# Routing of tokens to experts done sequence by sequence inside self attention, into a fixed region per expert

## The reference

```
x = x + cross_attention(layernorm(x), ctx, 8 heads of 64)
x = x + self_attention(layernorm(x), 8 heads of 128, 2 latent kv groups of rank 32)
xt = layernorm(x)                              # 1024 tokens x 512
probs = softmax(xt @ Wg)                       # 8 experts
topv, topi = top_k(probs, 2); topv /= sum(topv)
moe    = sum over the two chosen experts of topv * (gelu(xt @ Wu[e]) @ Wd[e])   # F = 1024
shared = gelu(xt @ W1) @ W2
x = x + shared + moe
```

## Time and profile before

| what | us |
|---|---|
| median of three runs | 1587.81 |
| profiled execution, own time | 1589.36 |
| profiled execution, span | 1587.5 |
| PE busy | 1516.4 (96%) |
| POOL busy | 720.5 (45%) |
| ACT busy | 686.3 (43%) |
| DVE busy | 625.6 (39%) |

### The profile page before, as it was taken

How to read it: one execution, slowest core, us unless ns; L and a number is a source line. 1 busy time by engine, 2 the same in 40 slices (tenths; PEclk the granted TensorE clock), 3 DMA queues, 4 the chain that set the end, 5 groups by cost and what they waited for, 6 DMA issues and landing times. The chain is left out here.

```text
span 1587.5 us, 25168 instructions
## 1 busy us (share of the span) xinstructions
PE 1516.4 (96%) x10038; PEld 1221.4 (77%) x10039; DVE 625.6 (39%) x953; ACT 686.3 (43%) x1121; POOL 720.5 (45%) x563
## 2 busy tenths in 40 slices
PE   7999999999999999999999999888699979999997
PEld 5678888888888888888888888745367768877876
DVE  4134434533534533632732731732654522222222
ACT  3244544544543544544543643504254424444621
POOL 3113822931941841851751651537200175688651
PEclk9999999999999999999999999999899989999999
DMA  6111021021021021021111111052000475467511
GB/s 212 60 54 59 2 87 44 18 87 34 28 87 34 28 87 34 28 75 39 35 60 54 34 41 54 1 194 92 15 1 1 153 226 146 140 190 195 146 35 35
DMA packets 56164, 116.90 MB, mean 74 GB/s; under 512 B 11072, under 2 KB 15232, under 8 KB 56064
## 3 DMA queue, kind: packets, MB, share of 16 engines
q1 hardware_dynamic: 46480, 98.17, 18.6%
q0 software_dynamic: 4816, 8.41, 2.8%
q10 hardware_dynamic: 4768, 8.91, 2.0%
HBM read 94.19 MB, written 22.33 MB: 73 GB/s over the span
## 5 line engine op out<-in xcount | busy, mean ns | idle before, releaser
L282 POOL TENSOR_TENSOR ctx_l<-stage,ctx_h 128x1024 fp32r<-128x1024 f32 x62 | 147.0, 2393 | 482.3 <-ACT ctx_h L630 482.3
L344 PE MATMUL ps_p<-wv,ctx_h 128*128 128x512 f32 x1024 | 323.7, 397 | 10.4 <-DVE ctx_l L700 9.4
L344 PE MATMUL ps_p<-ctx_h,wk 128*128 128x512 f32 x1024 | 331.0, 394 | 0.0
L738 DVE TENSOR_TENSOR s_top<-ps_s,s_top 128x512 f32<-128x512 f32 x192 | 121.2, 684 | 338.8 <-ACT s L599 338.8
L344 PEld LDWEIGHTS ps_p<-wv,ctx_h 128*128 128x128 f32 x1024 | 188.0, 189 | 53.7 <-issue 10.0
L344 PEld LDWEIGHTS ps_p<-ctx_h,wk 128*128 128x128 f32 x1024 | 192.2, 188 | 42.6 <-issue 1.2
L344 PE MATMUL ps_p<-wv,ctx_l 128*128 128x512 f32 x512 | 200.4, 391 | 0.0
L344 PE MATMUL ps_p<-ctx_l,wk 128*128 128x512 f32 x512 | 199.5, 390 | 0.0
L581 ACT ACTIVATE vt<-ps_p 128x512 f32<-128x512 f32 x128 | 76.4, 598 | 274.9 <-PE ps_p L344 213.7
L599 ACT ACTIVATE s<-ps_s 128x512 f32<-128x512 f32 x256 | 133.0, 602 | 61.1 <-PE ps_s L397 36.7
L575 ACT ACTIVATE kT<-ps_p 128x512 f32<-128x512 f32 x128 | 76.5, 598 | 176.7 <-PE ps_p L344 176.6
(11 more groups left out here) (255 smaller groups left out, 2253.9 us busy)
## 6 DMA issues: line engine op xcount, KB each, us to landing
stage<-in_ctx_dram SPq DMA_DIRECT2D x64, 512.0 KB, 4.0
raw_u<-in_up_dram SPq DMA_DIRECT2D x32, 512.0 KB, 4.2
stage<-in_down_dram SPq DMA_DIRECT2D x16, 512.0 KB, 4.1
raw_e<-in_down_dram SPq DMA_DIRECT2D x16, 512.0 KB, 4.1
rows_scratch<-wxo SPq DMA_DIRECT2D x25, 256.0 KB, 2.6
wxo<-rows_scratch ACTq DMA_DIRECT2D x23, 256.0 KB, 3.3
s<-in_x_dram SPq DMA_DIRECT2D x2, 1024.0 KB, 11.5
q_scratch<-s SPq DMA_DIRECT2D x2, 1024.0 KB, 4.6
```

The lines of the kernel that those rows point to most:

```text
L282: nc.gpsimd.tensor_tensor(lo, raw, hi, ALU.subtract).then_inc(done, 1)
L344: mm = nc.tensor.matmul(out, w(c), m(c), start=(c + k == 0), stop=(c == DC - 1 and k == 2))
L738: ins = nc.vector.tensor_tensor(top[:, p, e], bank, top[:, p, e], ALU.max)
```

## The change

- `EARLY` is 6, with a lag of its own: in step s the first half of shared tile `s - 1` and the second half of tile `s - 2` run, so tiles begin in step 1 where they began in step 3. `keys(1)` and `latents(1)` move to step 0. More raw buffers for the shared weights (parts of `wq`) keep the gelu's buffer free.
- A class `Routing` does the routing of sequence s - 1 in step s; the last sequence's is done in `experts`. The running counts are summed on POOL (`heap`).
- Each expert has a region of eight blocks of 128 rows in `rows_dram`, so a slot is `128 * 8 * expert + rank`. Two indirect DMAs per sequence send rows of 517 numbers: the 512 channels, the token, two weights, two experts. The 16 DMAs of tags and their table are gone. A table `where_i` maps tile number to block; ACT reads it for each load, DVE copies the tags out of the loaded rows (`take_tags`) and picks the weight (`choose_weight`).
- Cross attention fills all 66 blocks (517 wide, token number 1024), ten at the end of each b, from a buffer `blank`.
- The softmax's multiplication by the inverse sum moves from DVE (two instructions per sequence) to ACT (eight).
- The identity and the two masks for the ranks are set in self attention, not at the start of `experts`.

```diff
-ROWS = MAX_TILES + 2
+REGION = B * T // P
+ROWS = E * REGION + 2
-EARLY = 4
+EARLY = 6
+LAG = 1
@@ cross attention, SP
-                for n in range(B * T // P + (b - 1) * ZB, min(B * T // P + b * ZB, ROWS)):
-                    sp.dma_start(rows_dram[n], wxo[:, 0, :]).then_inc(zeroed, 16)
+                for n in range((b - 1) * ZB, min(b * ZB, ROWS)):
+                    sp.dma_start(rows_dram[n], blank[:, :]).then_inc(zeroed, 16)
@@ self attention, POOL, step s
                 if s < 2:
                     split(CH - 2 + s)
+                if s:
+                    routing.count(pool, s - 1)
+                    routing.scatter(pool, s - 1)
@@ self attention, PE
+            def rank(s):
+                await_empty(pe, f"rk{s}")
+                if s == 0:
+                    pe.wait_ge(on_set, 8)
+                pe.wait_ge(routing.both_done, s + 1)
+                pe.wait_ge(routing.heap_done, s + 1)
+                nc.tensor.matmul(bank(f"rk{s}")[:, 0:E], before, routing.both[:, s, :], start=True, stop=False)
+                fill(nc.tensor.matmul(bank(f"rk{s}")[:, 0:E], ones, routing.heap[:, s, :], start=False, stop=True),
+                     f"rk{s}")
@@ PE, step s
-                late, soon = s - EARLY, s - EARLY + 1
+                late, soon = s - LAG - 1, s - LAG
                 turn_probs(s)
                 if s + 1 < B:
                     scores(s + 1)
-                if late >= 0:
+                if 0 <= late < EARLY:
                     turn_gelu(late)
...
                 mix(s)
-                if late >= 0:
+                if s:
+                    rank(s - 1)
+                if 0 <= late < EARLY:
                     down_high(late)
                 if 0 <= soon < EARLY:
                     turn_norm(f"rowT{soon}", soon, B + soon + 1)
+                if s == 0:
+                    keys(1)
                 self_out(s)
-                if s == 1:
-                    keys(1)
-                if s == 2:
+                if s == 0:
                     latents(1)
@@ ACT, step s
                 take(f"pT{s}0", pT[:, 0])
+                if s:
+                    routing.exps(act, s - 1)
...
                 if s + 1 < B:
                     exps(s + 1)
...
+                if s + 1 < B:
+                    normalise(s + 1)
                 take(f"x3T{s}", x3T[:, s % 2])
@@ DVE, step s
                 if s + 1 < B:
                     maxes(s + 1)
+                if s:
+                    routing.choose(dve, s - 1)
                 take(f"u{s}", uT[:, :, :])
...
+                if s + 1 < B:
+                    invert(s + 1)
                 add(f"wo{s}", s)
...
                 norm(s, B + s)
-                if s + 1 < B:
-                    normalise(s + 1)
+                if s:
+                    await_filled(dve, f"rk{s - 1}")
+                    copy(nc.vector.tensor_tensor(routing.place[:, :], bank(f"rk{s - 1}")[:, 0:E], routing.base[:, :], ALU.add),
+                         f"rk{s - 1}")
+                    await_copied(dve, f"rk{s - 1}")
+                    routing.place_rows(dve, s - 1)
...
+                routing.largest(dve, s)
@@ class Routing: choose = max, max_index, copy of the two indices, compare,
@@ compare and add (both_done), then sum, reciprocal and multiply of the weights;
@@ place_rows = two picks, a reduce, a cast (slots_done)
+    def scatter(self, pool, s):
+        pool.wait_ge(self.tags_done, s + 1)
+        pool.wait_ge(self.slots_done, s + 1)
+        for k in range(2):
+            pool.indirect_dma_start(
+                out=self.rows_dram.rearrange("n p d -> (n p) d"),
+                out_offset=bass.IndirectOffsetOnAxis(ap=self.slot_i[:, k, s:s + 1], axis=0),
+                in_=self.xn3[:, s, :], in_offset=None).then_inc(self.added, 16)
@@ experts, SP
             load_raw(1)
-            sp.wait_ge(tags_set, 1)
-            sp.dma_start(meta_dram.rearrange("(p r) w -> p r w", p=P), pad[:, :, :]).then_inc(padded, 16)
-            for t in range(NT - 2):
-                store_out(t)
-            load_raw(2)
-            for t in range(NT - 2, NT):
+            for t in range(EARLY):
                 store_out(t)
             sp.wait_ge(added, 16 * 2 * NT)
-            sp.dma_start(tag[:, 0:MAX_TILES, :], meta_dram.rearrange("(r p) w -> p r w", p=P)).then_inc(tags_in, 16)
+            sp.dma_start(row[:, :], rows_dram[0]).then_inc(row_in, 16)
+            load_raw(2)
+            for t in range(EARLY, NT):
+                store_out(t)
@@ experts, POOL (the 32 indirect DMAs of rows and tags before are gone)
+            routing.scatter(pool, NT - 1)
@@ experts, PE: rank_last stands between the high and the low part of the up layer of tile 6
-            pe.wait_ge(consts, 9)
             turn(EARLY, xn3[:, EARLY, :])
-            tile(EARLY, 0, 0, rank_hits)
+            tile(EARLY, 0, 0, rank_last)
@@ experts, ACT
             def load_row(n):
-                act.dma_start(row[:, :], rows_dram[bass.ds(n, 1)].rearrange("o p d -> (o p) d")).then_inc(row_in, 16)
+                place = act.value_load(where_i[0:1, bass.ds(n, 1)], min_val=0, max_val=ROWS - 1)
+                act.wait_ge(tag_taken, n)
+                act.dma_start(row[:, :], rows_dram[bass.ds(place, 1)].rearrange("o p d -> (o p) d")).then_inc(row_in, 16)
@@ experts, DVE, tile 7 and routed tiles
+            weights_rest(range(DC))
+            hidden_rest(NT - 1)
+            row_rest(NT)
+            weights_rest(range(DC, CH))
+            dve.wait_ge(row_in, 16 * NT + 16)
+            take_tags(NT)
+            add_shared(NT - 1)
...
                 with dve.Fori(*bounds(dve, e)) as t:
+                    dve.wait_ge(row_in, t * 16 + 32)
+                    take_tags(t + 1)
                     hidden_rest(t)
                     row_rest(t + 1)
+                    choose_weight(t, e)
```

More of the change, by code:

```diff
@@ L1371, in exps, with normalise @@
                     copy(ins, f"sc{s}{g}")
+            def normalise(s):
+                par = s % 2
+                for g in range(SKV):
+                    act.wait_ge(inv_done, s * SKV + (g + 1))
+                    for r in range(REP):
+                        ins = nc.scalar.activation(sm[:, par, g, r, :], sm[:, par, g, r, :], ACT.Copy,
+                                                   scale=inv[:, par, g, r:r + 1])
+                    ins.then_inc(p_done, 1)
             for n in range(2):
@@ L1532, in experts @@
+def experts(nc, room, stage, on, up_ap, down_ap, out_ap, rows_dram, x2, xn3, logits, hu0, hd0, lu0, ld0,
+            rowT_h, rowT_l, gT_h, gT_l, raw_in, hi_done, lo_done, routing, added):
     with ExitStack() as ctx:
@@ L1573, in experts @@
         first_i = sb("first_i", [P, E + 1], U32)
-        slot = sb("slot", [P, 2, NT])
-        slot_i = sb("slot_i", [P, 2, NT], U32)
+        SEEN = MAX_TILES + 2
+        gap = sb("gap", [P, E - 1])
+        number = sb("number", [P, SEEN])
+        where = sb("where", [P, SEEN])
+        where_i = sb("where_i", [P, SEEN], U32)
+        passed = room[:, 0, 0:SEEN * (E - 1)].rearrange("p (t e) -> p t e", e=E - 1)
+        iota = routing.iota
         up_ps = ctx.enter_context(nc.psum_tensor("up_ps", [P, NH, 512], F32))
@@ L1829, in round_weights, with tile @@
                         .then_inc(hi_done, 1)
-            def tile(t, before_load=None):
+            def tile(t):
                 for n in range(NH):
@@ L1847, in _ @@
             act.sem_inc(row_in, 16 * NT)
-            act.wait_ge(route, 2)
-            nc.scalar.activation(probs[:, :, :], probs[:, :, :], ACT.Exp).then_inc(e_done, 1)
+            routing.exps(act, NT - 1)
             round_row(EARLY)
@@ L1852, in _ @@
             round_weights(1, None)
[L1853 removed]
+            for t in range(EARLY + 1, NT):
+                if t + 1 == NT:
+                    act.wait_ge(where_done, 1)
                 tile(t)
[L1856 to L1857 removed]
             act.wait_ge(firsts_done, 1)
@@ L1930, in _ @@
-            link(nc.vector.memset(first[:, 0:1], float(NT)))
-            hidden_rest(EARLY)
-            row_rest(EARLY + 1)
-            dve.wait_ge(counted, 1)
-            for t in range(NT):
-                link(nc.vector.tensor_tensor(earlier[:, t + 1, :], total_ps[:, t * E:(t + 1) * E], earlier[:, t, :],
-                                             ALU.add))
-            link(nc.vector.tensor_tensor(full[:, :, :], earlier[:, NT, :].unsqueeze(2).broadcast_to([P, E, NT - 1]),
+            dve.wait_ge(counted, 1)
```

376 lines of the change are left out of this document (210 added, 166 removed).

## The result

The changed kernel takes 1593.91 us, the median of 6 runs (1592.77 to 1595.16), against 1587.8 us of the kernel before beside it: a ratio of 1.0039, 95% interval 1.0026 to 1.0052. It is slower by more than the 0.2% that can be told. I had forecast 1576.3 us and a range up to 1587: both are wrong, and so is the side. On another chip the same two kernels gave 1594.66 and 1588.36 us, 1.0042 (1.0029 to 1.0055), so the loss is not that of one chip. The profiled execution took 1593.26 us with a span of 1591.4, where I had worked out 1577.9 and 1576.0.

A forecast was written before the change was run, and what follows sets the result against it. TensorE, busy 96% of the span, was taken as the bound, with a wait for tile 8's rows. The turn behind tile 8 was put at 1305.3, not 1316.86: 1587.81 - 11.5 = 1576.3 us; forecast 1571 to 1579, wider range 1563 to 1587.

The forecast's parts named there:

- Cross attention: Writing 66 blocks instead of 25 was to cost 0, with 7 us for each of six sequences as upper bound.
- Step 0: First step of self attention, with keys(1), latents(1) and ACT's eight multiplications: 18.0 us, from 15.5.
- The wait at the rank: Steps 2 to 6: TensorE stands 1.45 us for DVE's choose ahead of the rank matmuls; 20.4 us per step, from 18.70.
- Tile 8's rows in time: In experts, the rows of tile 8 land likeliest 22.5 us after the block's start, against 23.6 needed: no wait.
- rival B: Tile 8's rows come late in experts, with a wait of up to 6.5 us: 1579 to 1585 us; chance 0.15.
- Rival C: The new stop ahead of down_high drops the clock, 3 us lost each time; 1597 us with seven falls; chance 0.09.
- Step 1: Second step of self attention, with tile 0's up layer in and choose on the path: 18.8 us, from 16.2.
- Step 7 and the block's end: From step 7's start to the first turn of experts 15.6 us, TensorE starting at once after POOL's last scatter.
- Behind tile 8: In experts, expert 2's late weight chunks delay tile 8's gelu by 1.9 us; next turn 14.3 us later.
- The rest: Per routed tile, ACT's register read and DVE's tags and weight choice: 0, bounded by 0.3 us for each of 21 tiles.
- The mechanism of the gain: In experts, the 9.0 us wait for tile 8's rows goes, and 2.4 us of slow restart with it.
- rival A: The rank wait is filled or the early steps' clock lifted, up to 8.7 us back: 1565 to 1570 us; chance 0.20.

The follow-up runs named there:

- Experiment 1: Changed kernel, with DVE copying tile 8's tags ahead of the low parts of weight chunks 4 to 7: 1594.38 us.
- experiment 2: Changed kernel, with the weight choice's two scalar_tensor_tensor written as tensor_scalar; run twice, on two chips: second run 1592.35 us, 1.0018 to the kernel before.
- experiment 3: Changed kernel, with sequence 6's scatter issued at the start of experts, not at the end of self attention; run twice: second run 1592.18 us, 1.0017 to the kernel before.
- experiment 5: Changed kernel, with ACT normalising sequence 1 ahead of the copy of the values' second half in step 0: 1593.79 us, 1.0039 to the kernel before.
- experiment 6: Changed kernel, with the choice of experts behind the reciprocals on DVE and the rank matmuls behind the output matmuls: 1584.05 us, 0.998 to the kernel before.
- experiment 7: Changed kernel with all five edits (those of experiments 1, 2, 3, 5 and 6), run on two chips: 1577.08 us (0.993) and 1577.50 us (0.9927).
- the control: The changed kernel itself, unedited, timed again beside experiments 5 to 7 on another chip: 1594.66 us, 1.0042 to the kernel before.
- experiment 4: Changed kernel, with the two rank matmuls moved on TensorE from ahead of down_high to behind the row turn: 1593.74 us.

## Why the prediction was wrong

**Right.** Cross attention costs nothing. Step 0 (17.85 for 18.0; ACT's eight multiplications took 2.43 us for the 2.7 counted). The wait at the rank: 1.30 us for the 1.45 worked out, steps of 20.51 for 20.4. Tile 8's rows in time, rival B being wrong. Rival C, a fall of the clock in every step, is wrong too: the five waits of 1.30 us brought none (1.00 in the window of step 2; all of experiments 1 to 3 and 5 show one case), though it had the right side and was off by only 3 us in the time.

**Wrong, in four terms, all of them too small.**

*Step 1, 18.8.* "Followed operation by operation this gives 18.8 us": the text names no stretch of it at the lower clock. Its rank wait was 2.48 us, not 1.45, for there is no `down_high` and no tile before it. Windows show the clock at 0.50 from 1130 to 1136, behind the two waits of step 0, and again near 1140 to 1142 (0.53 from 1140 to 1143). In the kernel of experiment 6 with waits of 1.03, 1.24, 1.10 and 1.09 us and no second fall, the step took 19.71 us. With nearly the same waits ahead of a fall, in experiment 7, it took 22.01. One kernel shows it by itself: that of experiment 2 took 21.82 us in step 1 in its first trace and 24.42 in its second, where the second fall lasted longer and the clock fell a third time (0.61 from 1148 to 1152, 1.00 in the first trace). The first traces of experiments 1 and 3, whose edits don't touch step 1, have 24.40 and 24.42. So falls of the clock move step 1 by 2.3 to 2.6 us, with nothing changed in the work. The second fall of the changed kernel was a short one: TensorE is busy for 16.90 us of the step, 15.24 in experiment 6. So about 1.7 of the 3.3 us are the clock and 1.0 the longer rank wait; the rest is not taken apart.

*Step 7 and the block's end, 15.6.* "TensorE then starts at once": I let the block end with POOL's last instruction, 1.2 us behind the others. It ended 3.0 us behind POOL's last indirect DMA, and the experts started at the lower clock all the same. Experiment 3 took away 3.4 of the 3.9 us.

*Behind tile 8, 1.9 charged.* I followed the chunks, and not what stands ahead of the rounding in ACT's queue: a row load with a new wait, for a copy of DVE that stands behind 4.6 us of low parts. The tags are part of the change; my text had them under "the rest", at no charge. Experiment 1 puts 1.7 us on them, and leaves the other 1.9 to the chunk transfers that I had named and made too short.

*"The rest. ... I charge 0."* I had reasoned by room: DVE waits 4 us for each tile. It had the room, but an operation with two SBUF inputs, which the forecast had made one of "three small operations", stood for up to 5.15 us beside POOL's subtractions, past the end of the down layer. Experiment 2 gives back 2.5 of the 3.6 us.

The mechanism of the gain was right: the wait for tile 8's rows goes, and the turn of these rows comes 12.46 us behind the one before it, for 21.42. What made the side wrong is the sum: 14.4 us in these four terms, none of them the rank's wait of steps 2 to 6, which I had counted. Those five steps were also the largest cost of all, and the wait in them wasn't necessary. I took DVE's fixed order as a bound ("its order is fixed, with maxes first") and so gave rival A, a filled wait, as something that might happen by itself; it needed an edit, which gave 10.6 us in all, 5.1 of them in steps 2 to 6. That the kernel with all five edits comes out at 1577 us, near the forecast, is no support for the forecast: it lacks the rank waits that the forecast had in it.

What stays open: why the kernel before took 10 us more on one chip and whether the change loses there, and what decides whether the clock falls behind a wait of 1.1 us in step 1. With two to three us hanging on such falls, a forecast of that step is a choice between values, and 18.8 was below all of them (19.71 to 24.42 in the traces).

## What to carry to other kernels

When work is moved to a fuller place, follow each queue past every instruction that the moved part adds, waits for permission to overwrite included; an average of room says nothing about order. When a wait is put down to the place of one instruction, move that and look: if TensorE stops one instruction later for the same engine, that engine's order is the cause. Here a small operation with two SBUF inputs beside GpSimd's long ones cost 2.5 us and a block that ended on an indirect DMA 3.4: look for both in a trace, and write such an operation with one tensor input where it can be.

## What the runs showed of the hardware

- A SCALAR_TENSOR_TENSOR of 128x1 took 2.64 us in the mean of 21 and up to 5.15 beside GpSimd's TENSOR_TENSOR of 128x1024, of which one takes 2.96 us, so it can be held through more than one of them; a TENSOR_SCALAR with two scalars from SBUF, on the same data in the same place, took 0.27.
- Behind a block with an indirect DMA as GpSimd's last instruction the next began 3.00 us after it (2.79 to 2.90 in five more traces: the control and experiments 2, second run, 4, 5 and 6); with none there, in the second run of experiment 3, the next block began at 1271.35, 0.3 us after DVE's last operation (1270.92 and 0.15 us long).
- The same stretch, with nearly the same waits (1.24, then 1.10 us) ahead, at either level. The first window is of experiment 6, the second of 7 in its second run:

```profile
1143.00:1149.00 6.00, 4.91 (x27) 3.99 (x28) 5.28 (x9) 1.88 (x2) 4.42 (x4) 1.00 0.00 0
```
```profile
1143.00:1149.00 6.00, 5.64 (x15) 4.19 (x16) 4.98 (x7) 1.88 (x2) 4.58 (x4) 0.50 0.00 0
```

At 2.4 GHz TensorE did 27 matmuls there, at 1.2 GHz 15 (not wholly the same ones, since the first has come further). Waits of 1.30 us that recur every 20.5 us, with TensorE busy between them, brought one fall in 40: five of them in each of eight traces (the changed kernel twice, experiments 1, 2, 3 and 5, two of them twice), and only step 6 of experiment 1 was slower for it, 22.12 us at a clock of 0.63 from 1245 to 1249.
